# Attention values held stationary in column strips: turned softmax terms stream past them in batches of four units, and the reciprocal sums are applied where the terms are split in two halves

## The reference

```python
# layer 0: layer norm, scale and shift; latent K/V of rank 128; 16 heads of 32, 4 KV heads
scores = einsum('bhtd,bhsd->bhts', q, k_exp) / sqrt(32)
scores = where(mask, -inf, scores)          # window of 64, every 64th key, no future block of 128
y = einsum('bhts,bhsd->bhtd', softmax(scores), v_exp)
x = x + y.transpose(0, 2, 1, 3).reshape(B, T, 512) @ Wo.T
# layer 1: RMS norm, rope; 8 heads of 64, 1 KV head, no mask; then
h = ada_rms(x1, time_emb, ln2_w, ln2_tw)    # x1 = x + attention
out = x1 + (silu(h @ Wg.T) * (h @ Wu.T)) @ Wd.T    # inner width 2048
```

## Time and profile before

| | |
|---|---|
| median of 3 runs | 1804.08 us |
| the profiled execution, its span | 1804.9 us |
| TensorE busy | 1717.2 us, 95% |
| VectorE / ScalarE busy | 1152.3 us, 64% / 945.9 us, 52% |
| mean granted TensorE clock | 0.974 |
| chain that ended last, by engine | PE 77%, DVE 10%, DMA 6%, issue 4%, ACT 2% |

### The profile page before, as it was taken

One profiled execution on the slowest core, in us unless ns is written; L12 is line 12 of the kernel. 1 busy time (PEld: TensorE's weight loads), 2 busy tenths in 40 slices (PEclk: granted clock), 3 DMA queues, 4 the chain that ended last, 5 costly groups with the idle time before them and its releaser, 6 DMA issues.

```text
span 1804.9 us, 37773 instructions
## 1 busy us (share of the span) xinstructions
PE 1717.2 (95%) x12440; PEld 931.9 (52%) x12440; DVE 1152.3 (64%) x2858; ACT 945.9 (52%) x2769; POOL 398.8 (22%) x556
## 2 busy tenths in 40 slices
PE   6686899999999999999999999999999999999999
PEld 2344445555455545555455554555455554555444
DVE  6759566675667657685576756676576855767320
ACT  3836456364664538564483646645385644835320
POOL 3438587011111112111110111111121111101120
PEclk9676999999999999999999999999999999999999
DMA  7866489462784449662593637944485725936220
GB/s 245 152 181 115 126 197 253 98 117 82 163 175 94 80 119 184 133 118 78 127 194 91 119 88 161 171 95 82 115 192 125 123 73 138 196 85 112 100 70 24
DMA packets 527231, 234.30 MB, mean 130 GB/s; under 512 B 476336, under 2 KB 493744, under 8 KB 527024
## 3 DMA queue, kind: packets, MB, share of 16 engines
q1 hardware_dynamic: 511472, 175.09, 48.9%
q10 hardware_dynamic: 15552, 56.63, 10.1%
HBM read 90.09 MB, written 16.78 MB: 59 GB/s over the span
## 4 chain that ended last, share of the span: by engine, by line
PE 77%; DVE 10%; DMA 6%; issue 4%; ACT 2%; SPq 1%; DVEq 0%; POOL 0%; ACTq 0%
PE up L1427 8%; PE up L1429 8%; PE up L1428 8%; PE gate L1427 7%; PE gate L1429 7%; PE gate L1428 7%; PE y L1427 4%; PE y L1428 4%; PE y L1429 4%; PE bank L1427 4%; PE bank L1429 4%; PE bank L1428 4%; DMA prob_t<-prob 3%; PE bank L1454 2%; DVE prob L1113 2%
## 5 line engine op out<-in xcount | busy, mean ns | idle before, releaser
L864 ACT ACTIVATE bank<-bank,low 128x128 f32<-128x128 f32 (+2 forms) x768 | 302.7, 395 | 68.2 <-DVE low L1106 35.0
L702 POOL TENSOR_TENSOR inner_t<-inner,inner_t 128x512 f16<-128x512 f32 x128 | 149.0, 1164 | 662.7 <-ACT inner_t L1045 662.6
L1113 DVE TENSOR_TENSOR prob<-bank,prob 128x512 f16<-128x512 f32 (+1 forms) x320 | 202.8, 634 | 54.3 <-ACT prob L873 53.4
L873 ACT ACTIVATE prob<-bank 128x512 f16<-128x512 f32 (+1 forms) x320 | 178.7, 558 | 73.3 <-DMA prob_t<-prob 44.5
L1427 PE MATMUL up<-mlp,ring 128*128 128x512 f16 x512 | 194.9, 381 | 12.8 <-DVE inner L1392 12.8
L1382 DVE SCALAR_TENSOR_TENSOR silu<-silu,gate 128x512 f32<-128x512 f32 x128 | 87.9, 687 | 183.8 <-ACT silu L1039 183.0
L1427 PE MATMUL gate<-mlp,ring 128*128 128x512 f16 x512 | 194.0, 379 | 1.4 <-DVE mlp L1078 0.9
L1429 PE MATMUL up<-mlp,ring 128*128 128x512 f16 x512 | 194.9, 381 | 0.0
L1428 PE MATMUL up<-mlp,ring 128*128 128x512 f16 x512 | 194.9, 381 | 0.0
L1429 PE MATMUL gate<-mlp,ring 128*128 128x512 f16 x512 | 194.0, 379 | 0.0
L1428 PE MATMUL gate<-mlp,ring 128*128 128x512 f16 x512 | 193.9, 379 | 0.0
(11 more groups left out here) (182 smaller groups left out, 4041.8 us busy)
## 6 DMA issues: line engine op xcount, KB each, us to landing
ring<-wgu_dram ACTq DMA_DIRECT2D x108, 512.0 KB, 3.8
x_in<-x_dram SPq DMA_DIRECT2D x18, 512.0 KB, 3.8
x_res<-x_mid SPq DMA_DIRECT2D x16, 512.0 KB, 3.0
wgu_dram<-ring SPq DMA_DIRECT2D x16, 512.0 KB, 3.6
out_dram<-x_res SPq DMA_DIRECT2D x32, 256.0 KB, 2.3
prob_t<-prob SPq DMA_TRANSPOSE x256, 3.5
inner_t<-wd_t_dram SPq DMA_DIRECT2D x4, 1024.0 KB, 8.7
ring<-wg_t_dram SPq DMA_DIRECT2D x16, 256.0 KB, 4.1
```

The costliest lines, as they stand in the source:

```text
L702: pool.tensor_tensor(inner_t[:, 1, f, :], inner[:], inner_t[:, 0, f, :], ALU.subtract).then_inc(inner_low, 1)
L864: ins = act.activation(bank_[:, at:at + wid], bank_[:, at:at + wid], ACT.Exp, bias=low[:, j % BANKS, k:k + 1], scale=-1.0, accum_out=total)
L873: act.activation(terms(prob[:, g % SLOTS, 0, :], layer, j), terms(work_bank[USE[f"unit{layer}", j] % BANKS][:], layer, j), ACT.Copy).then_ ...
L1113: dve.tensor_tensor(terms(prob[:, slot, 1, :], layer, j), terms(work_bank[USE[name] % BANKS][:], layer, j), terms(prob[:, slot, 0, :], lay ...
```

## The change

- **Order of the units.** The four units of one `(s, t)` now stand in a row, and in tile 1 of layer 0 each holds heads of one KV group, so that four units (a batch, `BATCH`) hold the same heads of all KV groups.
- **Values.** `batch_values` replaces `unit_values`. V is the stationary operand, 32 columns (layer 0, four strips of the array) or 64 (layer 1, two strips), and the turned terms of four units move past it, 512 or 256 columns a matmul. Strip g writes partitions 32g on (or 64j on) of `ybank[s]`, so y comes out feature-major.
- **Reciprocal sums.** y can no longer be scaled by token, so the terms are. VectorE's `inverses` takes the reciprocal for each unit; `prob_highs` copies head by head with it as scale, and `prob_lows` multiplies and subtracts head by head. `normalise` and the fp32 transposes go; `heads` and `heads_low` split `ybank` directly.
- **Places.** Turned terms have eight places, four of them in `work`. Tile 0's projections stand inside the units (`OUT_AT`) and no longer after them. The rows of Wo of layer 0 are permuted on the host to the new order of heads, and Wo of layer 0 is split by POOL and no longer by VectorE in the first pair. `PLAN` is as it was.

```diff
-NORM_AT = [{LAST_OF[layer][s, 0] + LAG: s for s in BOTH} for layer in range(2)]
-FILL_AT = [{20: 0, 22: 1}, {12: 0, 14: 1}]
+BATCH = 4
+TAKE_AT = [{BATCH * last_batch(layer, s, 0) + BATCH - 1 + LAG + 1: s for s in BOTH}
+           for layer in range(2)]
+OUT_AT = [{14: 0, 18: 1}, {11: 0, 15: 1}]
...
-        SLOTS, TURNED = 3, LAG + 1
+        SLOTS, TURNED = 3, 2 * BATCH
...
-                need_apart(sp, pv_done, count(n, sum(UNITS), g - TURNED + 1), (cond_used, 1))
+                need_apart(sp, pv_done, count(n, sum(BATCHES), g // BATCH - 1), (cond_used, 1))
...
             def prob_highs(n, layer, j):
                 g = unit_index(layer, j)
-                need(act, terms_made, count(n, sum(UNITS), g + 1))
+                need(act, inv_ready, count(n, sum(UNITS), g + 1))
                 turned_before(act, n, g)
-                act.activation(terms(prob[:, g % SLOTS, 0, :], layer, j),
...
+                for h, at, wid in columns:
+                    ins = act.activation(prob[:, g % SLOTS, 0, at:at + wid], bank_[:, at:at + wid],
+                                         ACT.Copy, scale=inv[:, s, t, h:h + 1])
+                ins.then_inc(hi_done, 1)
...
             def prob_lows(n, layer, j):
...
+                for h, at, wid in columns:
+                    ins = dve.scalar_tensor_tensor(
+                        prob[:, slot, 1, at:at + wid], bank_[:, at:at + wid],
+                        inv[:, s, t, h:h + 1], prob[:, slot, 0, at:at + wid], ALU.mult,
+                        ALU.subtract)
+                ins.then_inc(prob_split, 1)
+
+            def inverses(n, layer, j):
...
+                need(dve, terms_made, count(n, sum(UNITS), unit_index(layer, j) + 1))
+                dve.reciprocal(inv[:, s, t, heads],
+                               (sums0 if layer == 0 else sums1)[:, s, t, heads]).then_inc(
+                                   inv_ready, 1)
...
                     prob_lows(n, layer, j)
                     if j + 2 < total:
                         lows(n, layer, j + 2)
...
+                    if j + 1 < total:
+                        inverses(n, layer, j + 1)
+                    if j in TAKE_AT[layer]:
+                        heads_low(n, layer, TAKE_AT[layer][j], 0)
+                    if j in OUT_AT[layer]:
+                        add(n, layer, OUT_AT[layer][j], 0)
...
+            HALVES = ((0, 0), (0, 1), (1, 0))
...
+                    for m, (rows, tile, places) in enumerate(blocks):
+                        for k, (of_v, of_p) in enumerate(HALVES):
+                            for g in range(KV0):
+                                ins = pe.matmul(
+                                    ybank[s][g * HD0:(g + 1) * HD0, out_cols],
+                                    v0[s][of_v][0:rows, tile, g * HD0:(g + 1) * HD0],
+                                    turned[0:rows, g, of_p, places, :], start=m == 0 and k == 0,
+                                    stop=m == len(blocks) - 1 and k == 2)
...
-                    if j in FILL_AT[layer]:
-                        heads(n, layer, FILL_AT[layer][j], 0)
-                    if j >= LAG:
-                        unit_values(n, layer, j - LAG)
+                    if j in OUT_AT[layer]:
+                        project(n, layer, OUT_AT[layer][j], 0, w)
+                    if (j - LAG) % BATCH == BATCH - 1 and j >= LAG:
+                        batch_values(n, layer, (j - LAG) // BATCH)
```

More of the change, by code:

```diff
@@ L90 @@
                 [use for j in range(UNITS[layer]) for use in (
[L91 to L92 removed]
+                    [(f"unit{layer}", j)] + [(f"heads{layer}", TAKE_AT[layer][k], 0)
+                                             for k in TAKE_AT[layer] if k == j])]
                 + [(f"heads{layer}", s, 1) for s in BOTH]
@@ L158 @@
 PIECE, DVE_PIECES = 512, 6
[L159 to L162, removed]
+PIECES_AT = {"first": range(0, 2), "lat.0": range(2, 6), "unit0_11": range(6, 7)}
+BIG = ["wo0", "wq1", "wo1"] + [f"wd{c}" for c in range(CH)]
+SPLIT_AT = {"fill0.0": BIG[:3], "kv1.0": BIG[3:6], "unit1_6": BIG[6:]}
 EARLY = 2
@@ L424, in build @@
             (key, w, p * PIECE, p * PIECE, PIECE) for key, w, pieces in (
-                ("wq0", wq0, 4), ("wo0", wo0, 4), ("wkv1", None, 1)) for p in range(pieces)]
+                ("wq0", wq0, 4), ("wkv1", None, 1)) for p in range(pieces)]
         def staged(key):
@@ L1456, in fill @@
                     ins.then_inc(full, 1)
-            def heads(n, layer, s, t):
-                bank_ = bank_for(n, f"heads{layer}", s, t)
-                need(pe, weighted, count(n, 8, 4 * layer + 2 * t + s + 1))
-                for c in range(CH):
-                    ins = pe.transpose(bank_[:, c * P:(c + 1) * P],
-                                       work[:, s, t, c * P:(c + 1) * P], ident[:])
-                ins.then_inc(full, 1)
             def token_major(out_ap, src, t, w, cols):
@@ new lines, in batch_values @@
+                        need(pe, low_made, count(n, LOW_USES, LOW_USE[f"heads{layer}", s, 0] + 1))
+                turned = turned_batch(batch_index(layer, b))
+                if layer == 0:
+                    heads = UNIT[0][first][2]
+                    out_cols = slice(heads[0][0] % 4 * P, (heads[-1][0] % 4 + 1) * P)
+                    blocks = ([(P, 0, slice(0, 4))] if t == 0 else
+                              [(P, 1, slice(0, 4, 2)), (K_NEAR, 2, slice(1, 4, 2))])
+                    for m, (rows, tile, places) in enumerate(blocks):
[6 more added lines that the diff above has]
+                                    stop=m == len(blocks) - 1 and k == 2)
+                else:
+                    for m in range(TILES):
+                        for k, (of_v, of_p) in enumerate(HALVES):
+                            for j in range(2):
+                                ins = pe.matmul(
+                                    ybank[s][j * HD1:(j + 1) * HD1, :], v1[s][of_v][:, m, :],
+                                    turned[:, :, of_p, 2 * j + m, :], start=m == 0 and k == 0,
+                                    stop=m == TILES - 1 and k == 2)
@@ L1539, in unit_values, with units @@
                 ins.then_inc(pv_done, 1)
-            def units(n, m, layer):
+            def units(n, m, layer, w):
                 total = UNITS[layer]
```

163 lines of the change are left out of this document (62 added, 101 removed).

## The result

The changed kernel takes 1997.72 us (median of 4 runs, 1996.95 to 2002.65) against 1803.69 us for the kernel before in the same series (1803.16 to 1806.08). The ratio is 1.108, with a 95% interval of 1.1064 to 1.1097. The direction was predicted and the stated range of 1860 to 2030 us holds the time, but the forecast of 1922 us is 76 us too low.

A forecast was written before the change was run, and what follows sets the result against it. TensorE bounds the kernel before; afterwards the ScalarE-VectorE ring decides. Layer 0's units +10.1, stretch behind -2.2, layer 1's units +8.1, stretch behind -1.3: +14.7 us a round, eight times 118, about 1922 us; range 1860 to 2030.

The forecast's parts named there:

- forecast case: Whole kernel: the ring costs more than TensorE saves, about 1922 us, own range 1865 to 1970; chance 0.66.
- serial strips: Rival, TensorE's value batches: strips run one after the other, 12.5 us a round over the forecast, about 2022 us; chance 0.16.
- The ring between ScalarE and VectorE: Units: high half, low halves, minima, reciprocal, next high half; turns 3.13 or 4.25, 2.09 or 3.20, layer 1 2.40 us.
- Strips together, transposes gone: TensorE: strips of a group share one stream and fp32 transposes go, so its work falls by 8.9 us a round.
- The mode changes: TensorE: 10 batches add 20 changes of tiling mode, up to 3.4 us a round, most where TensorE waits anyway.
- Window A: Units of layer 0: 58.5 us before, forecast 68.6, made of 66.4 in ring turns plus 2.2.
- narrow low half: VectorE's low-half piece for some columns of a unit: 0.20 us at 128 columns, 0.39 at 256.
- the allowance of 2.2: Units of layer 0: 2.2 us added to the summed turns for moments in which TensorE is late.
- Window B and D: Stretches behind the units of layers 0 and 1: 2.2 and 1.3 us a round shorter than before.
- The wait of 4.8 us: At each end of units, TensorE waits about 4.8 us for the last batch, and perhaps 3 more.
- the next 3.5 us at half clock: Rival, behind each end of units: clock falls for 3.5 us, 16 times, 56 us more, about 1978 us; chance 0.06.
- The ring hidden: Rival, units: turns hide behind TensorE's work and its saving comes through, 79 us less, about 1726 us; chance 0.10.

The follow-up runs named there:

- e2_recip_first: Changed kernel, all arithmetic kept, with VectorE's reciprocal of unit j + 1 ahead of the minima of unit j + 2: 1920.8 us (1.0646).
- e12_wide_no_ring_late: Changed kernel with wide copies and subtractions, no wait for the reciprocal, normalisation left out, tile 0's projections in the last two steps: 1767.5 us (0.98).
- e11_reorder_proj_late: Changed kernel with exponentials ahead of high halves, reciprocals ahead of low halves and gates, tile 0's projections in the last two steps: 1849.7 us (1.0255).

## Why the prediction was right or wrong

- *The time.* 1998 us lies outside the forecast case's own range, 1865 to 1970 us. The stated range holds it because it had been widened for the rivals, one of which (serial strips, 2022 us) did not happen. So the range was right in part by luck.
- *The ring between ScalarE and VectorE* was right: its order, its turns (each within 0.3 us) and its rank as the largest loss. Taking it apart by order gives 77 us (`e2_recip_first`).
- *Strips together, transposes gone* was right. But TensorE's side is worth at most 36 us (`e12_wide_no_ring_late`), half of the 8 x 8.9 = 71 us that the term had. The mode changes, which the sum left out, take some 1.8 us a round, 14 us. The rest is not divided.
- *Window A*, 68.6 us against 75.1 and 73.7. Two terms failed. The turns are 0.1 to 0.3 us longer, which over the 22 others is 3.7 us: I took 0.20 us for a narrow low half from a single instruction of the earlier trace rows, and four in a row take 0.26 each (757.34 to 758.38); for 193 columns I took 0.27, where a value between my own 0.20 and 0.39 is 0.30, and two take 0.33 each. (In layer 1 I likewise took 0.70 for two of 256 columns, where my 0.39 gives 0.78; they take 0.80.) And the projections were costed as 5.2 us of TensorE's work beside the ring, and the additions at nothing; in fact one projection stands in the ring, through the addition and the tanh behind it, and makes a turn of 8.15 us where 3.20 was forecast. The two make 8.7 us; the allowance of 2.2 took up a part. Late projections take A to 69.9.
- *Window B and D*, forecast 2.2 and 1.3 us shorter than before, came out 1.4 and 1.1 longer. The wait of 4.8 us was right (4.86), but "the next 3.5 us at half clock" had been kept in a rival of its own with a chance of 0.06. It came true **together with** the forecast case: the granted clock is 0.92 in B, 0.98 in D and 0.95 in A. Length times what is missing of the clock is 3.4 + 1.6 + 3.8 = 8.8 us a round, some 70 us in 8. That is an upper bound, since TensorE is also idle in a part of it, and in A a part lies beside the ring. B and D alone have 5.0 of it, 40 us in 8, of the 56 that the rival had as its price. No run takes the slow clock away and leaves the wait, so its share is worked out and not measured by itself. What to do otherwise: a stall that the sum already contains has its clock in the sum too, as rows of the first pair had shown.
- *The ring hidden* (1726 us) was wrong: even with both costs away the kernel took 1832 us, and 1767 with the projections moved too.

What stays open: the 82 us between `e11_reorder_proj_late` and `e12_wide_no_ring_late` are spread over all windows (2.5 and 2.8 us in the two shown, 9 to 13 us a round). No run divides them between the longer narrow instructions and what is left of the wait.

## What to carry to other kernels

Before moving a scale to an earlier step, follow who computes it: a factor that the last instruction of a unit's chain produces turns two pipelined engines into one ring, and then each narrow piece and each guest in their queues is paid in full. Where work is moved away, ask what it covered, and cover a wait with work that starts no transfer of its own: here the one cover that did so made the kernel 19 us slower, and the one that did not made it 41 us faster. A wait on TensorE can cost more than itself: behind one of 4.9 us, matmuls ran at 1.2 GHz for 6.4 us.

## What was unexpected

Strips overlap although the queue holds three matmuls of one strip in a row (0.78 us for twelve of 512 columns, where alternating strips take 0.76), and lose part of the overlap at six. And two costs that were 52 and 53 us when each stood alone were 166 together.
